# A mixture-of-experts layer on one NeuronCore: the width of an expert chosen in five places of TensorE's program instead of one

## The chip, the cores and the metric

One Trainium2 chip (trn2), one NeuronCore. The metric is the device time of one execution in microseconds. Three runs of the kernel before gave 617.49, 617.75 and 617.79 us, median 617.75.

## What is computed

x is 16 sequences of 128 tokens with 256 features in float32. Four blocks follow each other, each added to x through a tanh gate: a decaying retention over the context, a first mixture-of-experts layer, attention over the context, and a second mixture of experts. The change touches the first mixture of experts:

```python
def _moe_forward(x, Wg, W_in, W_out):            # E = 8 experts, K = 2 of them for a token, F = 512
    C = int(math.ceil(K * S / E * CAP_FACTOR))   # S = 2048 tokens: 640 places in each expert
    ...
    loc = jnp.take_along_axis(cum, flat_idx[:, None], axis=1)[:, 0]
    keep = loc < C
    buf = jnp.zeros((E, C + 1, h), x.dtype).at[e_flat, l_flat].set(xk)
    inp = buf[:, :C]
    hid = jnp.einsum('ech,ehf->ecf', inp, W_in)
    a, g = jnp.split(hid, 2, axis=-1)
    hid = jax.nn.gelu(a, approximate=False) * g
    out_e = jnp.einsum('ecf,efh->ech', hid, W_out)
```

## The kernel before, in words

Each engine has its own program, and they meet through semaphores. Layer 0 (the first mixture of experts) gathers the rows of each expert from DRAM into five tiles of 128 rows (POOL, `gather0`), turns them on TensorE (`xt0`), multiplies them with W_in (`hid0`) and the result with W_out (`out0`), and scatters the rows back (`scatter0`). Every product is made of three float32r matmuls over a high and a low part of both operands (`exact`, line 1542); ScalarE makes the high parts and VectorE the low ones.

On TensorE the eight experts are a loop of four passes with two experts in each (`Fori`, line 1616): par 0 has the even experts, par 1 the odd ones. `expert0` is one expert. An expert may have up to 640 rows, but if no more than 512 came to it, the last tile is empty and less work will do. So VectorE writes a flag for each expert into `full`; TensorE's queue loads the flag into a register (`value_load`, line 1607) and chooses between two copies of the expert's program:

- the wide copy: 8 hidden steps over 320 columns (12 matmuls each), and five output tiles of 12 matmuls;
- the narrow copy: 8 hidden steps over 256 columns, four output tiles of 12 matmuls, and one matmul for the fifth (line 1593), which only keeps the count of tiles.

In both copies the rows of the next expert are turned between the output tiles: tile 0, then the turned rows of pairs 0 and 1 (8 transposes), then tiles 1 and 2, then pair 2 (2 transposes, line 1554, which wait for VectorE to have read pair 0 of the same bank), then tiles 3 and 4. In memory the wide copy stands first and the narrow one behind it, and so for par 0, then for par 1. A wide expert runs its copy and jumps over the narrow one; a narrow expert jumps over the wide copy and goes on behind its own. Lines 1565, 1566, 1571, 1580, 1583 and 1584 are the waits in front of a step or a tile; where their count depends on the expert, they are register instructions in TensorE's queue.

```python
with pe.If(pe.value_load(full[0:1, bass.ds(e, 1)], min_val=0, max_val=1) > 0):
    run(HALF)
with pe.Else():
    run((CAP - P) // 2)
```

In this input experts 0, 3 and 7 are wide and 1, 2, 4, 5 and 6 narrow. Behind the loop TensorE goes on with the context of the attention, then the attention, then layer 1.

Of the kernel before, what the change touches and what calls it, by code (L numbers as in the profile page):

```python
# [30 lines left out]
P = 128  # L31
# [10 lines left out]
CAP = math.ceil(K * T / E * 1.25)  # L42
CT = CAP // P
# [5 lines left out]
HALF = CAP // 2  # L49
FB0 = F0 // P  # L50
FB1 = F1 // P
PIECES = 4
STEPS0 = 2 * FB0
# [47 lines left out]
def build(nc, x, ctxt, mask, g_xattn, g_ffn, wg0, w_in, w_out, wq, bq, wk, bk, wvT, wv, bvc, bv, wg1T, w1, w2, cf_d, out):  # L101
    with ExitStack() as ctx:
        def sb(name, shape, dt=F32):
            return ctx.enter_context(nc.sbuf_tensor(name, shape, dt))
# [80 lines left out]
        full = sb("full", [P, E], I32)  # L185
# [32 lines left out]
        def tiles_of(pair):  # L218
            return range(2 * pair, min(2 * pair + 2, CT))

        def bank0(pair):

            return PB[:, pair % 2, 0:len(tiles_of(pair)) * D].rearrange("p (t c n) -> p t c n", c=DC, n=P)
# [1164 lines left out]
        def _(pe):  # L1388
# [148 lines left out]
            def exact(dst, lhs_hi, lhs_lo, rhs_hi, rhs_lo, first=True, last=True):  # L1537

                n = len(lhs_hi)
                for k in range(n):  # L1540
                    for a, b in ((lhs_hi, rhs_hi), (lhs_hi, rhs_lo), (lhs_lo, rhs_hi)):
                        mm = pe.matmul(dst, a[k], b[k], start=(first and k == 0 and a is lhs_hi and b is rhs_hi),  # L1542
                                       stop=(last and k == n - 1 and a is lhs_lo))
                return mm


            def xt0(i, par, e, pair, between=None):
                if pair == 2:
                    pe.wait_ge(xt0_lo, e * PAIRS + 1)
                for t in tiles_of(pair):  # L1550
                    s = par * CT + t
                    pe.wait_ge(g0_in[s], i * 16 + 16)
                    for k in range(DC):
                        mm = pe.transpose(bank0(pair)[:, t % 2, k, :], xg[:, s, k * P:(k + 1) * P], ident)  # L1554
                    if t == tiles_of(pair)[-1]:
                        mm.then_inc(xt0_done, 1)
                    if between is not None:
                        between(t)

            def hid0(e, width):  # L1560

                for s in range(STEPS0):
                    half, fb = divmod(s, FB0)

                    pe.wait_ge(xt0_lo, e * PAIRS + PAIRS - 1 + half)
                    pe.wait_ge(hid0_used, e * STEPS0 + s + 1)
                    for n in range(2):
                        col = n * F0 + fb * P
                        for k in range(DC):
                            if s == 0 and n == 0:  # L1570
                                pe.wait_ge(win_lo[0], e * DC + k + 1)
                            mm = exact((PA, PC)[s % 2][:, n, 0:width],
                                       *([w[:, col + k * 2 * F0:col + k * 2 * F0 + P]] for w in (whi, wlo)),
                                       *([v[:, k, half * width:(half + 1) * width]] for v in (xhi, xlo)),
                                       first=k == 0, last=k == DC - 1)
                    mm.then_inc(hid0_done, 1)

            def out0(par, e, width, tiles_now):
                for t in tiles_now:
                    pe.wait_ge(wout_lo[0], e * 2 + 2)  # L1580

                    steps = FB0 if (t + 1) * P <= width else STEPS0
                    pe.wait_ge(h0_lo, e * STEPS0 + steps + 4)
                    pe.wait_ge(y0_evac, e * CT + t + 1)
                    bank = PD[:, (par * CT + t) % 2, 0:D]
                    if t * P < 2 * width:
                        at = t * P + (HALF - width) * (t * P // width)
                        exact(bank, *([h[:, f * CAP + at:f * CAP + at + P] for f in range(FB0)] for h in (hhi, hlo)),
                              *([w[:, WIN + f * D:WIN + (f + 1) * D] for f in range(FB0)] for w in (whi, wlo)))\
                            .then_inc(y0_done, 1)  # L1590
                    else:

                        pe.matmul(bank, hhi[:, 0:P], whi[:, WIN:WIN + D], start=True, stop=True).then_inc(y0_done, 1)

            def expert0(i, par, e):


                def run(width):
                    hid0(e, width)
                    out0(par, e, width, [0])  # L1600
                    xt0(i + par, 1 - par, e + 1, 0)
                    xt0(i + par, 1 - par, e + 1, 1)
                    out0(par, e, width, [1, 2])
                    xt0(i + par, 1 - par, e + 1, 2)
                    out0(par, e, width, range(3, CT))

                with pe.If(pe.value_load(full[0:1, bass.ds(e, 1)], min_val=0, max_val=1) > 0):
                    run(HALF)
                with pe.Else():
                    run((CAP - P) // 2)  # L1610

            for pair in range(PAIRS):
                xt0(0, 0, 0, pair, between=lambda t: values(1, [t]) if t < QB else None)
# [2 lines left out]
            with pe.Fori(0, E // 2) as i:  # L1616
                for par in range(2):
                    expert0(i, par, i * 2 + par)
# [190 lines left out]
```

## Time and profile before

| | |
|---|---|
| runs, median (lowest to highest) | 617.75 us (617.49 to 617.79) |
| profiled execution, its own time | 616.72 us |
| its span, first to last instruction | 614.7 us |
| mean granted TensorE clock | 0.921 of full speed |
| TensorE matmuls busy | 532.2 us, 87% |
| VectorE, ScalarE, POOL busy | 331.5, 304.0, 226.7 us |
| layer 0's experts on TensorE | from 81.70 to 251.9 us |

The span is what the profile shows; the execution's own time has 2.0 us around it. Times in the rows are microseconds from the span's start. PE is TensorE's matmuls, PEld its weight loads, and PEldq the queue that issues for both: register, wait and branch instructions stand there and are not counted as busy. The queue works ahead of the matmuls. "issue" is idle time for which the profile shows nobody to be waited for.

### The profile page before, as it was taken

What the parts mean: (1) busy time and instruction counts of PE and PEld (TensorE: products, weight loads), DVE (VectorE), ACT (ScalarE), POOL (GpSimd) and SP (SyncE); (2) the same over time, 40 slices, a digit from 0 to 9 for tenths busy, and PEclk for the clock granted to TensorE, in tenths of its full rate; (3) what the DMA queues carried; (4) which work ended last, traced back from release to release, by engine and by line L of the source; (5) the groups of instructions that cost most, each with busy time, mean ns of one, the idle gap of its engine ahead of it and who ended that gap; (6) DMA issues with size and microseconds to landing.
All of it is one profiled execution on the core that took longest, in us unless ns stands there. A gap on an engine that the chain in (4) does not pass through costs nothing.

```text
span 614.7 us, 12118 instructions
## 1 busy us (share of the span) xinstructions
PE 532.2 (87%) x3567; PEld 481.3 (78%) x3572; DVE 331.5 (54%) x817; ACT 304.0 (49%) x645; POOL 226.7 (37%) x256
## 2 busy tenths in 40 slices
PE   2796987899999999799891289999999999999991
PEld 1475877899999999777771178889898989898981
DVE  1878734356666675374858834544454445444520
ACT  3655335366656675426463435554555455545530
POOL 2300564345365450431000123535454435353531
PEclk9776599799999999979997579999999999999997
DMA  8943253144344434341122343645343544452231
GB/s 263 368 153 138 57 158 116 50 163 133 131 153 155 165 99 161 115 150 55 36 68 95 87 134 69 167 104 118 103 104 103 118 103 103 102 119 36 34 45 18
DMA packets 51726, 71.43 MB, mean 116 GB/s; under 512 B 7056, under 2 KB 43408, under 8 KB 51696
## 3 DMA queue, kind: packets, MB, share of 16 engines
q1 hardware_dynamic: 40752, 50.31, 24.8%
q0 software_dynamic: 10944, 20.76, 15.6%
q8 instruction: 14, 0.23, 0.2%
q14 instruction: 16, 0.13, 0.1%
HBM read 50.72 MB, written 20.33 MB: 116 GB/s over the span
## 4 chain that ended last, share of the span: by engine, by line
PE 70%; DVE 14%; issue 5%; ACT 3%; DMA 2%; SPq 1%; DVEq 1%; POOL 0%; ACTq 0%; POOLq 0%
PE PA L1542 25%; PE PD L1542 21%; PE PC L1542 8%; PE PC L1734 4%; PE PB L1399 3%; DVE stats L886 2%; PE PD L1399 2%; PE PB L1554 2%; DVE ys L1038 1%; DVE wlo L1159 1%; DMA xs<-x 1%; PE PA L1399 1%; ACT whi L746 1%; PE PB L1716 1%; PE PC L1399 1%
## 5 line engine op out<-in xcount | busy, mean ns | idle before, releaser
L1542 PE MATMUL PD<-whi,hhi 128*128 128x256 f32 x420 | 122.7, 292 | 0.0
L1542 PE MATMUL PD<-wlo,hhi 128*128 128x256 f32 x420 | 118.6, 282 | 0.0
L1542 PE MATMUL PD<-whi,hlo 128*128 128x256 f32 x420 | 118.5, 282 | 0.0
L554 POOL DMA_INDIRECT out<-ys,row_o x35 | 55.9, 1596 | 106.6 <-DVE ys L1350 106.3
L1542 PEld LDWEIGHTS PD<-wlo,hhi 128*128 128x128 f32 x420 | 80.1, 191 | 0.0
L1542 PEld LDWEIGHTS PD<-whi,hlo 128*128 128x128 f32 x420 | 80.1, 191 | 0.0
L1542 PEld LDWEIGHTS PD<-whi,hhi 128*128 128x128 f32 x420 | 79.9, 190 | 0.1
L481 POOL DMA_INDIRECT xg<-xn_rows,row_x x45 | 45.0, 1001 | 76.9 <-DVEq L1024 41.4
L844 ACT ACTIVATE hhi<-PC 128x512 fp32r<-128x512 f32 x70 | 38.1, 595 | 67.4 <-PE PC L1734 67.4
L534 POOL DMA_INDIRECT xg<-xn_rows,row_x x38 | 39.2, 1032 | 84.8 <-DMA xn_rows<-gate_rows 68.1
L839 ACT ACTIVATE xT<-PA 128x512 f32<-128x512 f32 x72 | 42.3, 599 | 49.8 <-PE PA L1542 49.5
L488 POOL DMA_INDIRECT y_rows<-ys,row_y x40 | 44.0, 1099 | 58.8 <-ACT ys L699 56.0
L1542 PE MATMUL PA<-whi,xhi 128*128 128x512 f32 x144 | 61.0, 423 | 2.9 <-DVE xlo L1159 2.9
L1542 PE MATMUL PA<-whi,xlo 128*128 128x512 f32 x144 | 57.4, 399 | 0.0
L1542 PE MATMUL PA<-wlo,xhi 128*128 128x512 f32 x144 | 56.8, 395 | 0.0
L1159 DVE TENSOR_TENSOR hlo<-PC,hhi 128x512 fp32r<-128x512 f32 x70 | 45.0, 685 | 14.5 <-ACT hhi L844 14.5
L1159 DVE TENSOR_TENSOR wlo<-raw,whi 128x512 fp32r<-128x512 f32 x64 | 40.0, 686 | 23.5 <-ACT whi L746 23.4
L1542 PE MATMUL PA<-xhi,whi 128*128 128x256 f32 (+1 forms) x128 | 38.7, 303 | 9.9 <-issue 7.3
L1350 DVE TENSOR_SCALAR ys<-PD,slot_gate 128x256 f32<-128x256 f32 x35 | 16.9, 484 | 52.7 <-PE PD L1542 45.4
L1159 DVE TENSOR_TENSOR xlo<-PB,xhi 128x256 fp32r<-128x256 f32 x37 | 15.7, 423 | 50.2 <-ACT xhi L834 48.2
L1122 DVE TENSOR_TENSOR ring<-ring,PA 128x320 f32<-128x320 f32 x32 | 15.6, 488 | 48.0 <-ACT ring L687 48.0
L1542 PE MATMUL PA<-xhi,wlo 128*128 128x256 f32 (+1 forms) x128 | 38.0, 297 | 0.0
(250 smaller groups left out, 1249.6 us busy)
## 6 DMA issues: line engine op xcount, KB each, us to landing
raw<-w SPq DMA_DIRECT2D x16, 1024.0 KB, 5.5
raw<-L_ffn_W_in SPq DMA_DIRECT2D x8, 1024.0 KB, 5.3
raw<-L_ffn_W_out SPq DMA_DIRECT2D x8, 512.0 KB, 3.6
y_rows<-ys SPq DMA_DIRECT2D x8, 512.0 KB, 7.1
xn_rows<-xn SPq DMA_DIRECT2D x8, 512.0 KB, 3.3
xs<-x SPq DMA_DIRECT2D x4, 512.0 KB, 7.8
cx<-ctx SPq DMA_DIRECT2D x4, 512.0 KB, 8.5
ys<-y_rows SPq DMA_DIRECT2D x4, 512.0 KB, 4.4
```

Source lines behind the costliest of these rows:

```text
L481: pool.indirect_dma_start(xg[:, s, :], None, xn_rows[0].ap(), bass.IndirectOffsetOnAxis(ap=row_x[:, e % E * CT + t:e % E * CT + t + 1], ax ...
L488: pool.indirect_dma_start(y_rows.ap(), bass.IndirectOffsetOnAxis(ap=row_y[:, e * CT + t:e * CT + t + 1], axis=0), ys[:, s, :], None).then_ ...
L534: pool.indirect_dma_start(xg1[j % 2], None, xn_rows[1].ap(), bass.IndirectOffsetOnAxis(ap=row_x[:, j:j + 1], axis=0)).then_inc(g1_in[j % 2 ...
L554: pool.indirect_dma_start(out, bass.IndirectOffsetOnAxis(ap=row_o[:, j:j + 1], axis=0), ys[:, j % 2, :], None, compute_op=ALU.add).then_in ...
L839: act.activation(h1[:, f * 512:(f + 1) * 512], PA[:, f, :], ACT.Silu).then_inc(silu_done, 1)
L844: act.activation(hhi[:, n * 512:(n + 1) * 512], PC[:, n, :], ACT.Copy).then_inc(ht1_hi, 1)
L1122: dve.tensor_tensor(ga[:, s % 4, :], ga[:, s % 4, :], (PA, PC)[s % 2][:, 1, 0:HALF], ALU.mult).then_inc(hid0_used, 1)
L1159: return dve.tensor_tensor(dst, src, hi.bitcast(F32), ALU.subtract)
L1350: dve.tensor_scalar(ys[:, par, :], PD[:, par, 0:D], slot_gate[:, bass.ds(j, 1)], None, ALU.mult)\
L1399: mm = pe.matmul(dst, a, b, start=(k == 0), stop=(k == len(lhs) - 1))
L1542: mm = pe.matmul(dst, a[k], b[k], start=(first and k == 0 and a is lhs_hi and b is rhs_hi), stop=(last and k == n - 1 and a is lhs_lo))
L1734: mm = pe.transpose(PC[:, n, b * P:(b + 1) * P], h1[:, f * P:(f + 1) * P], ident)
```

## The change

`hid0` gets the steps that it has to do as an argument. `expert0` loads the flag once and chooses by it in five places: hidden steps 0 to 3, hidden steps 4 to 7, output tile 0, output tiles 1 and 2, output tiles 3 and 4. The turned rows stand between them, once for both widths. The order of the matmuls of an expert stays as it was. The lines of the choice and the load are now 1598 (load), 1601 and 1607 (choices), and the loop is line 1625.

```diff
-            def hid0(e, width):
-
-                for s in range(STEPS0):
+            def hid0(e, width, steps_now):
+
+                for s in steps_now:
                     half, fb = divmod(s, FB0)
...
             def expert0(i, par, e):
 
 
-                def run(width):
-                    hid0(e, width)
-                    out0(par, e, width, [0])
-                    xt0(i + par, 1 - par, e + 1, 0)
-                    xt0(i + par, 1 - par, e + 1, 1)
-                    out0(par, e, width, [1, 2])
-                    xt0(i + par, 1 - par, e + 1, 2)
-                    out0(par, e, width, range(3, CT))
-
-                with pe.If(pe.value_load(full[0:1, bass.ds(e, 1)], min_val=0, max_val=1) > 0):
-                    run(HALF)
-                with pe.Else():
-                    run((CAP - P) // 2)
+                wide = pe.value_load(full[0:1, bass.ds(e, 1)], min_val=0, max_val=1)
+
+                def hidden(steps_now):
+                    with pe.If(wide > 0):
+                        hid0(e, HALF, steps_now)
+                    with pe.Else():
+                        hid0(e, (CAP - P) // 2, steps_now)
+
+                def output(tiles_now):
+                    with pe.If(wide > 0):
+                        out0(par, e, HALF, tiles_now)
+                    with pe.Else():
+                        out0(par, e, (CAP - P) // 2, tiles_now)
+
+                hidden(range(FB0))
+                hidden(range(FB0, STEPS0))
+                output([0])
+                xt0(i + par, 1 - par, e + 1, 0)
+                xt0(i + par, 1 - par, e + 1, 1)
+                output([1, 2])
+                xt0(i + par, 1 - par, e + 1, 2)
+                output(range(3, CT))
```

TensorE's program, before, at the end of the narrow copy of par 0, where par 1 begins: the last output tiles, the load of the flag, and the one choice, behind which the wide copy starts (PD holds the output tile, PA and PC the hidden products).

```order
L1593 MATMUL PD<-whi,hhi 128x256
L1609 UNCONDITIONAL_BRANCH
L1607 ISA
L1607 TENSOR_LOAD full
L1607 ISA x2
L1607 COMPARE_AND_BRANCH
L1565 ISA
L1566 ISA
L1571 ISA
```

With the change the same boundary has the same instructions (lines 1598 and 1601 for 1607), but the choice now jumps over four hidden steps, 48 matmuls of 320 columns, where it jumped over the whole wide copy of 166.

TensorE's program, before, narrow copy, from the end of output tile 2 over pair 2 of the turned rows to tile 3:

```order
L1542 MATMUL PD<-wlo,hhi 128x256
L1542 MATMUL PD<-whi,hlo 128x256
L1549 ISA
L1554 MATMUL PB<-cf,xg 128x128 x2
L1584 REGISTER_ALU
L1542 MATMUL PD<-whi,hhi 128x256
```

The same place with the change (the narrow piece; the wide piece of tile 3 and 4 stands in the same way behind the choice):

```order
L1542 MATMUL PD<-wlo,hhi 128x256
L1542 MATMUL PD<-whi,hlo 128x256
L1609 UNCONDITIONAL_BRANCH
L1549 ISA
L1554 MATMUL PB<-cf,xg 128x128 x2
L1607 COMPARE_AND_BRANCH
L1580 ISA
L1583 ISA
L1584 ISA
```

A branch has come in between the turned rows and the tile, and three register instructions (ISA) stand where a wait and one register instruction (REGISTER_ALU) stood.

## Rows read from the trace of the kernel before

**Rows 1.** The page, parts 1 and 3: busy time by engine, and the instruction queue.
```profile
PE 532.2 (87%) x3567; PEld 481.3 (78%) x3572; DVE 331.5 (54%) x817; ACT 304.0 (49%) x645; POOL 226.7 (37%) x256
...
q8 instruction: 14, 0.23, 0.2%
```

**Rows 2.** Stretches of layer 0, PE alone: stretch, length, busy (count), clock, DMA share, GB/s.
```profile
104.31:110.56 6.25, 0.00 (x0) 0.80 0.57 218
110.56:115.59 5.03, 5.03 (x26) 0.57 0.01 3
131.67:134.81 3.14, 3.14 (x26) 1.00 0.89 273
150.38:172.71 22.33, 22.33 (x167) 1.00 0.41 131
...
191.62:210.77 19.15, 18.72 (x155) 1.00 0.47 151
...
110.56:131.67 21.11, 20.61 (x155) 0.90 0.23 70
```

**Rows 3.** The chain of waits around the start of expert 1: start, length, what.
```profile
104.31 6.25 issue
...
115.59 1.44 PE PA L1542 x12
```

**Rows 4.** Timeline of VectorE, 101 to 103: expert 1's last operand.
```profile
102.36 0.42 DVE L1115 TENSOR_TENSOR xlo<-PB,xhi 128x256 fp32r<-128x256 f32 x1
```

**Rows 5.** Line 1607 in five short stretches: ns min/median/max, first and last start.
```profile
L1607 PEldq COMPARE_BRANCH  x1: 3306/3306/3306, 102.0 to 102.0; - x1
...
L1607 PEldq COMPARE_BRANCH  x1: 4047/4047/4047, 106.2 to 106.2; - x1
...
L1607 PEldq COMPARE_BRANCH  x1: 169/169/169, 170.7 to 170.7; - x1
...
L1607 PEldq COMPARE_BRANCH  x1: 208/208/208, 191.0 to 191.0; - x1
...
L1607 PEldq COMPARE_BRANCH  x1: 77/77/77, 229.0 to 229.0; - x1
```

**Rows 6.** DMA queues in 87.8:88.8, 102.9:103.9, 107.8:108.8 and 110.9:112: packets, MB.
```profile
q8 instruction: 1, 0.02, 5.7%
...
q8 instruction: 1, 0.02, 6.0%
...
q8 instruction: 1, 0.02, 6.1%
...
q8 instruction: 1, 0.02, 5.4%
```

**Rows 7.** All instruction queues in 116.8:253.8 (q14 is not TensorE's).
```profile
q14 instruction: 3, 0.02, 0.1%
```

**Rows 8.** The stretch between two code packets: PE and PEld busy (instructions), the other engines.
```profile
87.90:103.00 15.10, 15.10 (x117) 15.10 (x116) 9.57 (x18) 8.99 (x21) 6.46 (x7) 1.00 0.22 62
```

**Rows 9.** Timeline of the weight loads: the first of expert 4, behind expert 3.
```profile
172.71 0.19 PEld L1542 LDWEIGHTS PA<-xhi,whi 128*128 128x128 f32 x1
```

**Rows 10.** Lines 1565 and 1571 in 191:191.6, behind a taken choice.
```profile
L1565 PEldq FUSED_REGOPS  x1: 42/42/42, 191.3 to 191.3; - x1
L1571 PEldq FUSED_REGOPS  x1: 37/37/37, 191.5 to 191.5; - x1
```

**Rows 11.** How far the queue is ahead in expert 4: register and wait instructions, then matmuls.
```profile
L1583 PEldq EVENT_SEMAPHORE  x1: 51/51/51, 182.8 to 182.8; - x1
184.35 0.28 PE L1542 MATMUL PD<-whi,hhi 128*128 128x256 f32 x1
...
L1583 PEldq EVENT_SEMAPHORE  x2: 51/51/51, 189.2 to 189.5; - x2
189.68 0.36 PE L1542 MATMUL PD<-whi,hhi 128*128 128x256 f32 x1
```

**Rows 12.** Waits of the weight loads in 111:252: total us, times, longest.
```profile
PEld PA L1542 <- issue: 2.0, 5, 0.7
```

## The prediction, made before the changed kernel ran

> **What bounds the kernel now.** I first read the page: TensorE (PE) is busy 87% of the span, VectorE 54%, ScalarE 49% [rows 1]. That is an average, so the table of stretches comes next, cut at the eight experts of layer 0 [rows 2]. In each of the experts 1 to 7 the matmul time fills the stretch to within 0.5 us; three of the rows stand for them: wide expert 3 is 22.33 us of matmuls back to back, narrow expert 5 takes 19.15 us with 18.72 busy, expert 1 21.11 with 20.61. Nothing that VectorE, ScalarE or a transfer does shows in this stage; whatever delays TensorE there delays the end.
>
> Between expert 0 and expert 1 it stands still. The chain of waits has one piece named "issue" of 6.25 us at 104.31, the longest of the stage [rows 3], and the granted clock tells what follows: expert 1 begins at 0.57 mean, so at the 1.2 GHz level for most of its first 26 matmuls, which take 5.03 us, where the same 26 matmuls of expert 2 take 3.14 us at 1.00 [rows 2, 3]. No data is missing: the last operand of expert 1, xlo, was written from 102.36 on, for 0.42 us [rows 4].
>
> The rows of line 1607 say what "issue" is. Two branches are long: the jump from the end of the wide copy over the narrow one, 3306 ns from 102.0, and the choice that sends expert 1 to its narrow copy, 4047 ns from 106.2. The same jump after expert 3 takes 169 ns, and the same choice 208 ns for a narrow and 77 ns for a wide expert [rows 5]. In the middle of both long branches the instruction queue q8 moves one packet, 0.02 MB, at 102.9 to 103.9 and at 107.8 to 108.8 [rows 6]. So both branches waited for code. From 116.8 to 253.8 q8 moves nothing, though the loop runs three more times [rows 7]: the loop's code, once there, stays. The loss belongs to the first pass alone.
>
> How far apart is the code? Between the packets of 87.8 to 88.8 and of 102.9 to 103.9, TensorE ran 117 matmuls and 116 weight loads [rows 6, 8], with some 14 register and wait instructions by the program, so a packet carries about 250 instructions (estimate). Counting two instructions for a matmul, the jump of expert 0 passes over the narrow copy, 155 matmuls or 336 instructions, and the choice for expert 1 over the wide copy, 358 instructions. Both distances are more than one packet.
>
> **Removed.** The five choices cut the same program into pieces of at most 104 instructions; the longest jump is now one of these. A piece ahead is therefore in the packet that runs or in the next one. That the next is fetched ahead also after a jump shows behind the second long branch: q8 moves a packet at 110.9 to 112 [rows 6], while expert 1 still has some 80 instructions to go to the end of the packet it jumped into. From entering a packet to needing the next, the first pass has at least 5 us, and the longest wait for code is 4.05 us. So I take both long branches at their later values, 169 and 208 ns. Behind expert 3, also wide and followed by a narrow one, the first weight load of expert 4 has no idle time in front of it [rows 9]. The 6.25 us go down to 0.1 us: **-6.15 us**. Without standstill the clock has no reason to fall, as at none of the later boundaries [rows 2]: 5.03 becomes 3.14, **-1.89 us**. Together -8.04.
>
> **Added: four more choices for each expert.** A choice costs the queue that issues for TensorE about 0.3 us when taken (208 ns, and the next register instruction stands 0.3 us behind, 191.0 to 191.3), and each piece sets three registers for its waits, 0.1 us each (the first at 191.3, the third at 191.5) [rows 5, 10]; before, one or two such instructions stood there, 0.2 us. So 0.4 us in a narrow expert and, with 77 ns not taken, about 0.2 in a wide one. Whether TensorE feels it depends on how far its queue is ahead:
> - Behind the hidden products the wait of output tile 0 stands in the queue at 182.8, its first matmul runs at 184.35 [rows 11]. The lead is 1.6 us, a little more than one hidden step (12 matmuls in 1.44 us [rows 3]). The choices in front of tile 0 and of the second half of the hidden steps, 0.4 us each, are hidden.
> - Between the turned rows and output tiles 1 and 2 the queue has the 1.44 us of tile 0 and 0.87 us of turns to run ahead. Hidden.
> - In front of tile 3 it is not. The queue waits there for the last turned rows' bank, and is back at 189.2, 0.4 us ahead of the matmul at 189.68 [rows 11]. From there to the next expert it is the queue that sets the pace, since tile 4 of a narrow expert has one matmul: even now the five boundaries behind a narrow expert leave up to 0.7 us open, 2.0 us in all [rows 12]. So 0.4 us for each narrow expert: five times, **+2.0 us**. A wide expert has 24 matmuls there, 2.9 us to catch up: about 0.1 us each, three times, **+0.3 us**.
>
> The bounds of that term: nothing, if the lead covers all; and 1.0 us for a narrow and 0.3 for a wide expert, if the choice in front of tiles 1 and 2 shows too with its registers: 5.9 us. I take 2.3, by the rows at 189. The shared turned rows cost nothing and save nothing in time: each expert ran one copy of them anyway. The loop's code shrinks by 20 matmuls of 1400 instructions; nothing follows from that. The other engines' programs are the same, and they are ready: POOL, VectorE and ScalarE wait for TensorE in this stage. What comes behind the loop starts when TensorE gets there, so the gain stays.
>
> **Sum.** -8.04 + 2.3 = -5.7 us. The profiled execution took 616.72 us (span 614.7 and 2.0 around it), 1.0 us under the median of the three runs, 617.75. So 611.0 for a profiled execution, and **612.0** for the median.
>
> The Trainium skill bears on this in "Runtime: NRT & Kernel Launch", section "Instruction fetch mechanics". It says that code comes in blocks of 16 KiB, 256 instructions, and that TensorE's memory holds 2048; the trace agrees with the first (q8: 14 packets, 0.23 MB, on the page [rows 1]), and with the second as far as a loop of 1400 instructions stays. "Advanced Engine Details and Errata", section "ISA Cache", says "Only 2 cache lines!"; by that every pass of the loop would fetch again, the even flow of experts 2 to 7 would be impossible, and the loss to win would be far more than 8 us. The trace decides against it for TensorE [rows 7].
>
> **Rivals.**
> *The choices show (slower).* If no choice is hidden, 4 more of them in 8 experts are 32, and at 0.4 us more for 20 and 0.3 us for 12 they cost 11.6 us; with the branch at the end of each wide piece (169 ns, 12 times, 2.0) 13.6. Net +5.6: **623.3**. For it: the last boundary shows that the lead can be as small as 0.4 us. Against: the lead of 1.6 us inside the hidden products [rows 11]. The point where it decides is 8.04 / 32 = 0.25 us for each added choice.
> *Jumps stop the fetching ahead (slower).* Then each new packet of the first pass is waited for: five of them within the two experts, each up to 4.05 us less a lead of 1.6, about 2.5 us, so 12.3 us in place of 6.15, the clock still falls, and the choices cost their 2.3: +8.5, **626.2**. For it: the long jump ended at 105.3, and no packet followed before the choice of 106.2 asked for one. Against: the packet of 110.9, and that choice came within 0.8 us.
> The same page of the Trainium skill states it as a rule: prefetch is purely sequential, and "branching breaks sequential prefetch", which is why it would have straight code. By that rule five choices are worse than one, and this rival would be the likely one; a run of before shows only one packet that speaks against it.
> *Half of it.* One of the two waits for code stays somewhere in the first pass, behind a boundary of packets that I place only within 30 instructions. It leaves 2.5 us open, as above, and may keep the clock down: -8.04 + 2.5 + 1.89 + 2.3 = -1.35, **616.4**; with the clock kept up, -3.2, 614.5.
> *No gain.* The 6 us come back as a wait behind the loop. Nothing in the rows speaks for it, since each later stage starts from TensorE's end.
>
> **Chances.** The forecast 0.68, half of it 0.12, the choices show 0.10, no fetching ahead 0.06, no gain 0.04. A measurement of this kernel tells 0.2%, 1.2 us, from no change. Faster by more: forecast and half, 0.80; within: 0.05; slower: 0.15. The range starts at 609.4, where the choices cost nothing (617.75 - 8.04 = 609.7, and 0.3 for the runs' spread), takes in the forecast with the highest price of the choices (617.75 - 8.04 + 5.9 = 615.6) and the half case, to 616.5. What lies outside, the slower rivals and no gain, is 0.20.
>
> **What the profile would show.** Right: no branch over 0.3 us in the expert stage, eight choices and four times as many more at 208 or 77 ns; between expert 0 and 1 under 0.5 us; clock 1.00 from expert 0 to the end of the stage; the same number of q8 packets, 14, none of them within a long branch; narrow experts about 0.4 us longer, from the first to the last 5.7 us shorter. Wrong: a branch of 3 or 4 us left in the first two experts (half, or no fetching ahead), or gaps of 0.2 to 0.6 us in front of the second half of the hidden products and of output tiles 0 and 1 (the choices show).

## The result, and the profile after

The changed kernel takes **612.21 us** (median of 6 runs, 609.38 to 614.46), the kernel before it, run beside it, 617.33 us (6 runs). The ratio is 0.9927, 95% interval 0.9898 to 0.9956. In two more comparisons, each on a chip of its own and with 5 to 19 runs a side, the same pair gave 0.9887 [0.9855, 0.9919] and 0.9916 [0.9885, 0.9947]. In microseconds the three differences are 5.1, 8.1 and 4.1, mean 5.8, where 5.7 was forecast. Each has an interval of about 2 us to both sides, so the closeness of the mean is in part luck. The sum behind the forecast did not come out: one term of it turned out to be nothing, and in each of the three pairs of profiles 1.9 to 2.9 us are given back behind the stage, in a place that the prediction didn't name.

The profiled execution took 609.38 us. Its page, parts 1 and 3, against [rows 1]:
```profile
PE 536.6 (88%) x3567; PEld 484.5 (80%) x3572; DVE 332.7 (55%) x817; ACT 303.5 (50%) x645; POOL 227.1 (37%) x256
...
q8 instruction: 14, 0.23, 0.2%
```
TensorE has the same 3567 matmuls, and the instruction queue moves the same 14 packets.

The two groups of choices in the first expert layer: line 1601 chooses for the hidden steps, line 1607 for the output tiles (ns min/median/max):
```profile
L1601 PEldq COMPARE_BRANCH  x21: 73/208/313, 82.4 to 232.1; - x21
L1607 PEldq COMPARE_BRANCH  x33: 65/183/337, 89.8 to 240.5; - x33
```
54 branches, none over 0.337 us (a 55th, the first of all, ends before the stage starts and is short too). The 3306 and 4047 ns of [rows 5] are gone.

The chain of waits around the start of expert 1 (start, length, what), against [rows 3]:
```profile
97.04 0.22 PE PB L1554 x2
97.26 2.88 PE PD L1542 x24
100.13 1.44 PE PA L1542 x12
```
The piece of 6.25 us named "issue" is gone too, and expert 1's first hidden step takes 1.44 us at once, as that of expert 2 did before.

The experts, one stretch each (length, PE busy, count, clock, DMA share, GB/s), against [rows 2]:
```profile
99.97:119.77 19.80, 19.02 (x158) 1.00 0.42 145
119.77:139.12 19.35, 18.95 (x155) 1.00 0.48 150
139.12:161.57 22.45, 22.45 (x168) 1.00 0.44 131
```
In these three the clock stays at 1.00. In expert 0 it does not (23.99 us at a mean of 0.93, where 1.00 was forecast): it is at half its level from 77.1 to 80.5, which before didn't have and which costs about 1.5 us, as shown below. The whole stage, 75.98 to 242.76, takes 166.8 us against 170.4 before (81.70 to 252.06 there): 3.6 us gained in this pair of profiles, not 5.7. Three things were therefore open: whether distance is what made the two branches long, whether the choices cost something (narrow expert 2 takes 19.35 us here and 18.71 in the trace of before), and where the rest is.

### The profile page after: what moved, and what is told of

Its sections match the earlier page's. It is cut to its first block, busy times and chain, and to the rows that moved or that the text cites. A ratio compares the mean times of both kernels' runs of the same rounds, so it can differ in the third digit from the quotient of the medians.

```text
span 607.4 us, 12186 instructions
## 1 busy us (share of the span) xinstructions
PE 536.6 (88%) x3567; PEld 484.5 (80%) x3572; DVE 332.7 (55%) x817; ACT 303.5 (50%) x645; POOL 227.1 (37%) x256
## 4 chain that ended last, share of the span: by engine, by line
PE 67%; DVE 17%; issue 6%; ACT 4%; DMA 2%; SPq 1%; DVEq 1%; POOL 0%; POOLq 0%; ACTq 0%
PE PA L1542 24%; PE PD L1542 21%; PE PC L1542 8%; PE PC L1743 3%; DVE stats L886 3%; PE PB L1399 2%; PE PD L1399 2%; PE PB L1554 2%; DVE ys L1038 2%; DVE xs L1173 1%; DVE wlo L1159 1%; PE PB L1725 1%; PE PA L1399 1%; DMA xs<-x 1%; DVE xs L1209 1%
## 5 line engine op out<-in xcount | busy, mean ns | idle before, releaser
L1542 PE MATMUL PC<-xhi,whi 128*128 128x256 f32 (+1 forms) x128 | 38.1, 297 | 0.4 <-DVE ring L1122 0.4
```

## The experiments

Theory: a branch is long when it goes to code further off than the packet fetched ahead, and only in the first pass. Rival for the branches: any rearrangement of the code would do. Rival for the choices, which is the prediction's term: each narrow expert pays 0.4 us for them.

### One choice, but the narrow copy first

```diff
-                with pe.If(pe.value_load(full[0:1, bass.ds(e, 1)], min_val=0, max_val=1) > 0):
+                with pe.If(pe.value_load(full[0:1, bass.ds(e, 1)], min_val=0, max_val=1) < 1):
+                    run((CAP - P) // 2)
+                with pe.Else():
                     run(HALF)
-                with pe.Else():
-                    run((CAP - P) // 2)
```

> One choice per expert as before, but the narrow copy stands first in the program and the wide one behind it. Theory (code): the long branches of the first pass come from jumping over more than the next packet of code. Expert 0 is wide and now runs the second copy, so its end falls straight into the load for expert 1, and expert 1 is narrow and goes straight on. No branch over 0.3 us, no standstill at expert 1, clock 1.00 there: the stage of the eight experts takes 170.4 - 8.0 = 162.3 us, each narrow expert 18.7 to 19.2 us as before, and the time is about 609.5 us. Rival (first use): code that runs for the first time costs its wait wherever it stands, or the standstill has another cause at that moment (the weights' transfers). Then a standstill of 4 to 6 us stays between expert 0 and 1 and the time stays within 2 us of 617.3.

Measured: 616.45 us, ratio 0.9976 [0.995, 1.0002], so nothing that can be told from no change, where about 609.5 had been expected. The long branches between experts 0 and 1 are gone as expected (the longest is 368 ns), but the chain of waits has a new piece inside expert 0:
```profile
81.33 0.53 PE PC L1542 x2
81.86 2.54 issue
84.40 2.83 PE PC L1542 x10
87.23 2.81 PE PA L1542 x12
```
TensorE stands still in the second hidden step, and the next 22 matmuls run at the half level of the clock, where it had been since 79.2. The jump into the wide copy is at 77.7. TensorE can run 14 matmuls of it and then lacks code, so the jump landed close to the end of a packet, and the next packet begins only at 81.9. The table of stretches says what the DMA engines did meanwhile (PE, PEld, DVE, ACT, POOL busy; clock, DMA share, GB/s):
```profile
78.00:79.00 1.00, 0.59 (x4) 0.59 (x5) 0.00 (x0) 0.00 (x0) 1.00 (x1) 1.00 0.98 397
79.00:80.00 1.00, 1.00 (x6) 1.00 (x5) 0.00 (x0) 0.00 (x0) 1.00 (x2) 0.60 1.05 430
...
81.00:82.00 1.00, 0.86 (x4) 0.73 (x3) 0.17 (x1) 0.44 (x1) 1.00 (x1) 0.50 1.11 373
82.00:83.00 1.00, 0.00 (x0) 0.00 (x0) 0.32 (x1) 0.00 (x0) 0.25 (x1) 0.50 0.11 28
```
They are full with the weights of the next expert until 82, and the packet moves when they are through. My expectation had looked at distance alone. This gave a second cause to test: the packet waits behind the weights.

### More and fewer choices

Three kernels on the same chip divide the work otherwise. Hidden steps whole, so four choices for an expert:
```diff
-                hidden(range(FB0))
-                hidden(range(FB0, STEPS0))
+                hidden(range(STEPS0))
```

> The change with one choice for all eight hidden steps, so four choices per expert. In the changed kernel each narrow expert stands still 0.57 us in the second half of its hidden steps, where the signal of one step (hid0_done) comes 1.1 us behind its last matmul instead of 0.3. Theory: that delay comes with the choice in the middle of the hidden steps. It goes: narrow experts 18.7 to 18.9 us where the changed kernel has 19.4 to 19.8, the stage 2.9 us shorter, about 609.3 us. Rival: every choice costs its share in the queue, 0.65 us over four added ones: narrow experts 0.16 us shorter only, 0.8 us in all. The pieces of 206 instructions are still shorter than a packet, so no long branch.

Two choices, one around the hidden steps and one around all outputs, which have the turned rows in each copy again:
```diff
+                def outputs(width):
+                    out0(par, e, width, [0])
+                    xt0(i + par, 1 - par, e + 1, 0)
+                    xt0(i + par, 1 - par, e + 1, 1)
+                    out0(par, e, width, [1, 2])
+                    xt0(i + par, 1 - par, e + 1, 2)
+                    out0(par, e, width, range(3, CT))
...
+                for part in (lambda w: hid0(e, w), outputs):
```

> Two choices per expert: hidden steps, and all output tiles with the turned rows inside both copies. Longest jump 206 instructions. Theory (code): no branch over 0.4 us in the first pass, no standstill at expert 1, and nothing late in the hidden steps: narrow experts as before (18.7 to 19.2 us), about 609.3 us. Rival: pieces of this length reach the end of the packet sooner than the next one is there, so that one branch of 1 us or more stays in experts 0 or 1, about 611.

The hidden steps in four, so seven choices:
```diff
-                hidden(range(FB0))
-                hidden(range(FB0, STEPS0))
+                for s in range(0, STEPS0, 2):
+                    hidden(range(s, s + 2))
```

> The change with the hidden steps in four pieces of two, so three choices inside them instead of one. Theory (a choice inside the hidden steps delays a signal): each of the three costs a narrow expert up to 0.57 us: narrow experts 20.0 to 21.1 us, wide ones as before since their steps leave 0.3 us more; the stage 3 to 6 us longer than the changed kernel's, 615 to 618 us. Rival (the delay belongs to one step of the expert, whatever the choices): narrow experts stay at 19.4 to 19.8 us and the time at 612.

Measured, beside 617.22 us for before:

| choices | time | ratio | experts' stage | longest branch |
|---|---|---|---|---|
| 2 | 610.59 | 0.9888 [0.9842, 0.9934] | 167.6 us | 2624 ns |
| 4 | 608.21 | 0.9862 [0.9817, 0.9906] | 168.4 us | 2167 ns |
| 7 | 609.91 | 0.9889 [0.9845, 0.9933] | 166.8 us | 337 ns |

The intervals overlap, and the three can't be ranked. Two readings follow. Two and four choices still leave one long branch, so not every rearrangement does it, and the rival written down for the kernel with two choices is what came. The branch is the choice of expert 1's hidden steps, behind the load of its flag; line 1609 in the kernel with two choices, and the instruction queue in 99.8:100.71, just before it starts:
```profile
L1609 PEldq COMPARE_BRANCH  x2: 286/1455/2624, 99.5 to 100.7; - x2
```
```profile
q8 instruction: 1, 0.02, 9.8%
```
In 100.71:103.4, while it waits, the queue moves nothing. So the packet that it waits for was on its way before the branch began, and the branch jumps over 206 instructions only, less than a packet. Distance is not the cause of this one. It is time: the jump of 286 ns before it had just entered a packet, at 99.8, the next packet starts 0.8 us later, at 100.6, and is of use only at 103.3. In the kernel with four the packet starts at 99.6 and the branch of 2167 ns at 100.15. TensorE stands still for 1.9 and 1.2 us there, where it was 6.25 in before.

And seven choices are not slower than four, where 615 to 618 us had been expected. The branches of the kernel with seven (44 at the hidden steps, where the change has 21):
```profile
L1601 PEldq COMPARE_BRANCH  x44: 67/188/312, 78.9 to 235.4; - x44
L1607 PEldq COMPARE_BRANCH  x33: 65/179/337, 93.2 to 243.8; - x33
```
The narrow experts 2, 4 and 6 take 19.4 to 19.5 us in the three kernels, and 19.6 to 19.8 in the one with a single choice on the same chip. That is 0.7 over the 18.7 of expert 2 in the trace of before, but it does not grow with the number of choices. My expectation for the kernel with four, that the delay would go, failed too. Their waits name the place, in the kernel with seven:
```profile
PE PA L1542 <- DVE ring L1122: 1.7, 4, 0.5
PE PA L1542 <- issue: 0.6, 2, 0.3
PE PC L1542 <- DVE ring L1122: 0.4, 1, 0.4
```
Once in each narrow expert, inside the hidden steps, the hidden products wait for VectorE (the two rows with it, five times in all). In the trace the semaphore of the fifth hidden step arrives there 1.0 to 1.15 us behind the start of the step's last matmul, and that of every other step 0.3 us. Whether the change has any part in that needed before and after side by side.

### Before and after, twice more

The two kernels unchanged, on a second and on a third chip.

> The kernel before, unchanged, profiled together with the runs below. In the first profile of it no hidden step stood still, while the changed kernel and four variants of it, also the one with a single choice (e1), stand still 0.5 to 0.6 us once in each narrow expert. Theory (the choices cost it): here too no standstill inside the hidden steps, narrow experts 18.7 to 19.2 us. Rival (it belongs to the execution, not to the change): 0.5 to 0.6 us in the hidden steps of the narrow experts here as well, 19.3 to 19.9 us each, and then the added choices cost next to nothing. In both: two long branches of 3 to 4 us between expert 0 and 1.

> The changed kernel, unchanged, beside it: no branch over 0.4 us in the expert stage, expert 0 to 1 without standstill, clock 1.00 from expert 1 on, eight experts in 165 to 167 us; 6 to 9 us less than the stage of the kernel before in the same call. The time 0.987 to 0.993 of before.

> The kernel before, unchanged, as the partner of the two kernels beside it on the same chip. Ratio 1.000, 614 to 617.5 us; between expert 0 and expert 1 two long branches of 3.3 to 4.1 us, the first expert layer 169.5 to 171 us. It also tells apart two readings of the 0.5 to 0.6 us standstill inside the hidden steps of each narrow expert: if it belongs to the chip or the execution, it shows here whenever it shows in the changed kernel beside it; if the small choices made it, it never shows here (narrow experts of 18.7 us).

> The changed kernel, unchanged. My theory by now: no long branch in the first expert layer, the added choices cost nothing that can be measured, so about 8 us less than before: ratio 0.986 to 0.991, the layer 162 to 164 us. The rival, the reckoning of the prediction with 0.4 us for each narrow expert: 5.7 us less, ratio 0.991, the layer 164 to 165.5 us with narrow experts of 19.1 to 19.4 us while the kernel before beside it has 18.7.

The first of these two is called the second chip below (the four kernels above ran on one chip of their own, and which chip the first pair ran on isn't on record). There: before 613.73, after 606.65, ratio to the 19 runs of before (614.72) 0.9887 [0.9855, 0.9919]. Narrow expert 2, before and then after:
```profile
128.57:147.28 18.71, 18.71 (x155) 1.00 0.49 155
```
```profile
122.47:141.16 18.69, 18.69 (x155) 1.00 0.49 155
```
Third chip: before 616.32, after 612.28, ratio to the 19 runs of before (616.39) 0.9916 [0.9885, 0.9947]. The same expert, before and then after:
```profile
128.90:148.24 19.34, 18.97 (x155) 1.00 0.46 150
```
```profile
122.88:142.23 19.35, 18.99 (x156) 1.00 0.47 150
```
This settles the choices. On the second chip neither kernel has the wait inside the hidden steps, on the third **both** have it, also the kernel without the added choices. It belongs to the chip or the execution. And within one chip the lengths of the narrow experts 2, 4, 5 and 6 are the same in both kernels to 0.06 us. Over experts 2 to 7 on the third chip, where 24 choices were added, before takes 122.73 us (the lengths 19.34, 22.44, 19.30, 19.75, 19.29 and 22.61) and after 122.70; on the second 120.38 and 120.23. The added choices cost 0.0 us, to about 0.1. The stage's length missed the ranges written down for it: 163.35 us in after on the second chip (165 to 167 expected), and 172.97 and 164.88 on the third (169.5 to 171, and 162 to 164). So did the ratio on the third chip, 0.9916 where 0.986 to 0.991 had been written down for a cost of nothing.

The stage on the third chip takes 172.97 us before and 164.88 after: **8.1 us** less, of which 6.35 in expert 0 with the standstill behind it and 1.71 in expert 1. On the second it is 6.6 us. There the first stretch of after's expert 0 shows why it isn't 8.1; the second row is the third chip's:
```profile
79.35:103.33 23.98, 23.98 (x166) 0.93 0.37 116
```
```profile
80.70:103.15 22.45, 22.45 (x167) 1.00 0.42 111
```
On the second chip the clock was at half its level from 80.6 to 84.0, just behind the start of the stage, which costs 1.5 us. Of the twelve profiles told of here without the block of the next section, six have such a stretch: the first of after, this one, the kernels with four and with seven choices, the one with the narrow copy first, and the kernel before with a late transfer, below. That is four of six with added choices and two of six with a single one, too few to say whether the choices have a part in it.

### A distance of more than a packet, put in on purpose

238 matmuls that never run are set between the hidden steps and output tile 0 of even experts, so that a choice must jump over 477 instructions in each pass. The bound of the flag's load is raised to 2, so that the new condition isn't decided beforehand:
```diff
-                wide = pe.value_load(full[0:1, bass.ds(e, 1)], min_val=0, max_val=1)
+                wide = pe.value_load(full[0:1, bass.ds(e, 1)], min_val=0, max_val=2)
...
+                if par == 0:
+                    with pe.If(wide > 1):
+                        for n in range(238):
+                            pe.matmul(PD[:, 0, 0:D], hhi[:, 0:P], whi[:, WIN:WIN + D], start=True, stop=True)
```
The flag is 0 or 1, so nothing that is computed changes.

> The changed kernel with a piece of 238 matmuls (477 instructions) that never runs, between hidden products and output tile 0 of the even experts. Theory (code packets of 256 instructions, the next one fetched when one is entered): the jump over it goes from instruction 1006 to 1484, two packets on, right after the packet of 1006 was entered, so in expert 0 it waits about 3 us: one branch of 2.5 to 4 us at 90 us, of which 1 to 2.5 us show on TensorE. The loop is then eight packets long: if eight stay, experts 2, 4 and 6 show nothing; if not, the same branch is long again in each of them. Rival (the long branches of before had to do with the load of the flag or with the change of expert, not with distance): no branch over 0.4 us anywhere.

Measured in a single execution: 643.43 us against 614.72. The jump over the block (line 1615), the loop's jump back (line 1629) and the instruction queue:
```profile
L1615 PEldq COMPARE_BRANCH  x4: 208/5048/6240, 90.1 to 244.1; - x4
```
```profile
L1629 PEldq COMPARE_BRANCH  x3: 3437/3457/3637, 124.6 to 223.7; - x3
```
```profile
q8 instruction: 36, 0.59, 0.4%
```
The first of the four, in expert 0, took 6240 ns, where after has no branch over 0.337 us: in the first pass a distance of more than a packet is enough to make a long branch, since nothing but never-run code was added. It is more than the 2.5 to 4 us expected; two packets move meanwhile, the first only 2.2 us into it, and why so late is open. Those in experts 2 and 6 took 5163 and 4933 ns, but the one in expert 4 took 208 ns over the same distance, and no packet moves from 182 to 219: a far jump costs nothing when the code is there. The block did more than I wanted, since the loop, now some 1850 instructions long, no longer stays as a whole: 36 packets instead of 14, and a wait of 3.4 to 3.6 us at each turn of the loop. The 29 us are therefore not the price of four jumps, and the run says nothing on that price.

### Does the packet wait behind the weights?

First in the kernel before: the transfer of expert 2's W_in, which fills the DMA engines during the second long branch, is held until expert 1 has done its second hidden step.
```diff
+                    if e == 2 and first:
+                        sp.wait_ge(hid0_done, STEPS0 + 2)
```

> The kernel before, with the transfer of expert 2's W_in (1 MB, issued at 102.5, in the middle of the standstill) held back until expert 1's second hidden step is done. Theory (the code packet queues behind the weights on the DMA engines: in before it starts at 107.9, when they fall idle, 1.7 us after it was wanted): both branches stay long, but the second takes 2.5 to 3.1 us instead of 4.05 and the standstill is 1 to 1.5 us shorter; stage and time 1 to 2 us shorter. Rival (fetching code takes 3 to 4 us by itself): both branches as before, the time the same.

Measured: 612.38 us, ratio 0.9976 [0.9941, 1.001], not to be told from none. The branches show what the time doesn't (line 1609 here is line 1607 of before):
```profile
L1609 PEldq COMPARE_BRANCH  x2: 2107/2904/3701, 101.1 to 105.8; - x2
```
The second branch falls to 2107 ns, from 4047 [rows 5], and from 3407 on the same chip. The standstill falls from 6.1 to 4.8 us; waits of TensorE in 98:112, the kernel before and then this one:
```profile
PE PA L1542 <- issue: 6.1, 1, 6.1
```
```profile
PE PA L1544 <- issue: 4.8, 1, 4.8
```
So some 1.3 us of the second long branch was the packet's turn in the DMA engines.

This trace also shows what the second branch waits for. It starts at 105.8. The instruction queue in 104.8:105.77, before it:
```profile
q8 instruction: 1, 0.02, 6.3%
```
In 105.77:107.9, while it waits, the queue moves nothing. So here too the target lay in a packet already on its way, which starts 0.75 us behind the end of the first long branch, and not in one further off. In before the same packet starts 2.6 us behind the end of the first long branch, in its two repeats 2.1 and 2.2, with the DMA engines at a share of 1.0. In all four the branch ends 1.3 to 1.4 us after the packet has moved. The first long branch is another case: its packet starts about 1.0 us after the branch does. So of the two, the first is the one that distance made long. The second is long because it comes about 1 us after a packet was entered, while the next is of use only 3.0 us after that, or 4.4 to 4.9 us with the weights in the way.

Then the sharper test: the kernel with one choice and the narrow copy first, with the weights out of the way of the packet that came late there. SyncE issues in order, so W_out's transfer, behind W_in's, is held too; both are issued after 82 there.
```diff
+                    if e == 1 and first:
+                        sp.wait_ge(hid0_done, 3)
```

> The kernel with one choice around all products and the narrow copy first, which stood still for 2.5 us in expert 0's second hidden step, with one thing more: the transfer of expert 1's W_in is not started until expert 0's third hidden signal. Theory (the packet of code waited in the DMA engines behind the transfers of the weights): with the weights out of the way the packet arrives at 79 to 80 us instead of 82, the standstill shrinks to under 0.5 us, TensorE's clock doesn't fall to half again after it, and the time is 607 to 610 us, ratio 0.986 to 0.991, with a single choice. Rival 1 (the packet is late by the instructions' own fetching, whatever the DMA engines carry): the standstill stays at 2 us or more and the time at ratio 0.996 to 1.000, as without the wait. Rival 2: the other transfer (W_out, issued 0.5 us later on the same engines) holds the packet as long; then too the standstill stays, and the DMA engines' share stays near 1 to 82 us.

Measured on the third chip: **609.25 us, ratio 0.9899 [0.9864, 0.9935]**, with a single choice, where it had 0.9976 without the wait (on another chip). The stretches and the chain around the old standstill:
```profile
78.00:79.00 1.00, 1.00 (x9) 1.00 (x8) 0.00 (x0) 0.00 (x0) 0.98 (x2) 1.00 0.22 57
79.00:80.00 1.00, 0.96 (x7) 0.84 (x6) 0.00 (x0) 0.29 (x1) 1.00 (x1) 1.00 0.47 86
80.00:81.00 1.00, 0.45 (x4) 0.45 (x4) 0.49 (x1) 0.14 (x1) 1.00 (x2) 1.00 0.04 12
```
```profile
79.67 0.29 PE PC L1544 x2
79.96 0.59 issue
80.55 1.62 PE PC L1544 x10
```
The packet moves at 78.1, 1.2 us behind the jump and at a DMA share of 0.2, instead of 4.2 us behind it at a share of 1.0; the standstill falls from 2.54 to 0.59 us (under 0.5 had been expected), and the clock stays at 1.00 (part of the gain may be that the stage here began without the half-clock stretch of 79.2, which the transfer can't be shown to have caused). The theory holds for the packet and the standstill. Rival 1 is out. Rival 2, W_out by itself, was not told apart, since both transfers moved.

One small thing remains for the single choice. With the narrow copy first, a narrow expert ends on a jump over the wide copy, just in front of the load of the next expert's flag. Its narrow experts 2, 4 and 6 take 19.72, 19.54 and 19.70 us, those of before and after on that chip 19.29 to 19.35.

## Why the prediction was right, and where it was not

**What bounds.** Right. TensorE's queue waited for code in two branches. The instruction queue, the distance put in, and the late transfer all say so. What it missed is that it put both branches down to a distance of more than one packet. That holds for the first. The second jumped into the packet that was already coming, and waited because it came too soon after the first, and 1.3 us longer because the weights were in the DMA engines. The change removes both cases, and so the price of the removal held.

**Removed: -6.15 and -1.89.** Right. On the third chip, where no half clock falls at the start of the stage, the stage loses 8.09 us: 6.35 in expert 0 with the standstill, 1.71 in expert 1, and 0.03 in all others. The forecast was 6.15 and 1.89, together 8.04. In the other two pairs the stage lost 3.6 and 6.6 us. 1.5 us of the difference is each time the half clock in expert 0, where 1.00 was forecast; about 3 us more in the first pair are the late semaphore in the narrow experts, which its profile of after has and its profile of before has not.

**Added: +2.3.** This is the step that failed. The prediction put the choice in front of tile 3 behind the wait at 189.2, with the queue 0.4 us ahead, and took 0.4 us for each narrow expert. It measured 0.0. The wait at line 1583 that I read there as that for the turned rows' bank is that of the output tiles, which stands *behind* the choice in the program. In after the choice (line 1607) is taken at 181.7 and a wait of line 1583 comes at 182.3, while the last matmul of tile 2 starts at 181.84; the third chip's rows:
```profile
L1607 PEldq COMPARE_BRANCH  x1: 208/208/208, 181.7 to 181.7; - x1
```
```profile
L1583 PEldq EVENT_SEMAPHORE  x1: 51/51/51, 182.3 to 182.3; - x1
```
From tile 1's first matmul to the next expert's first it is 4.97 us there (179.00 to 183.97) and 4.98 before (185.01 to 189.99). And the queue comes to the load of the next expert's flag at the same moment in both, 3.59 us behind tile 1's first matmul; before, then after:
```profile
L1607 PEldq FUSED_REGOPS  x2: 51/101/151, 188.6 to 189.1; - x2
```
```profile
L1598 PEldq FUSED_REGOPS  x2: 37/94/151, 182.6 to 183.1; - x2
```
Between its last wait and that load the queue has nothing of its own to do for 0.53 us in before and for 0.13 us in after: the choice costs the queue the 0.4 us that I had reckoned, but it had them to spare, although it was only 0.4 us ahead of tile 3. So the wrong step is the sentence that from there on the queue sets the pace. From the load of the flag to the next first matmul it is 1.27 us before and 1.28 after, which the change didn't touch. What holds the queue in that gap no row tells. The lower bound that the prediction gave for this term, "nothing, if the lead covers all", is the value.

**"The gain stays."** Only in part, in the three pairs of profiles. Something is given back behind the stage each time. From the end of the stage to the first scores' products of the following attention (line 1666 of before, 1675 of after) the two kernels take:

| profiles | before | after |
|---|---|---|
| first pair | 28.4 us | 32.1 us |
| second chip | 28.8 us | 30.3 us |
| third chip | 27.9 us | 32.2 us |

The work is the same. The chain of waits on the third chip, before:
```profile
256.53 5.52 PE PD L1399 x32
...
262.42 1.68 DVE xs L1173 x4
...
264.12 2.09 DVE xs L1173 x4
...
274.03 3.70 PE PB L1399 x8
```
And after:
```profile
250.46 7.01 PE PD L1399 x32
...
257.84 2.39 DVE xs L1173 x4
...
260.26 2.50 DVE xs L1173 x4
...
270.57 5.40 PE PB L1399 x8
```
5.52 becomes 7.01 and 3.70 becomes 5.40: these are stretches in which the granted clock is at its half level, 250.4 to 260.6 and 270.9 to 274.3 in after, only 258.2 to 265.0 in before. VectorE's eight operations take 1.1 us more; why is open. Together 4.3 us. Before has a half-clock stretch at 306.0 to 309.4 that after lacks, so up to the second expert layer the loss is 2.6 us (103.4 against 106.1 us from stage to stage; 1.9 in the first pair and 2.9 on the second chip). The kernels with two, four and seven choices take 101.1 to 103.5 us there and so don't show it, though their stages end at about the same time. So it isn't a price of short choices as such. Nor is it a matter of when the stage ends: that is 245.6 in after on the third chip, which shows the loss, and in the kernel with four choices, which doesn't. Chance in three profiles is not ruled out.

**Sum.** Stage and what lies behind it, up to the second expert layer, come to -1.7 us in the first pair of profiles (-3.6 and +1.9), -3.7 on the second chip (-6.6 and +2.9) and -5.5 on the third (-8.1 and +2.6), where the medians of the runs differ by -5.1, -8.1 and -4.1. So a pair of profiles doesn't give the difference of the runs: one profile stands for one execution, and the one of after on the second chip, 609.22 us, is the slowest of its five. The prologue alone varies as much: the stage starts at 81.7, 79.0 and 78.7 in before and at 76.0, 79.4 and 80.7 in after. What can be said is that the forecast's -8.04 was right for an execution without the half clock in expert 0, that its +2.3 stood at the wrong place, and that the match of 5.7 and 5.8 is luck so far as it rests on what happens behind the stage, which nobody had reckoned.

**Rivals.** "The choices show": out, 8 x 7 choices are as fast as 8 x 4. "Jumps stop the fetching ahead": out. After has five packets within the first two experts, and no branch waits for any; behind the second long branch of before, which ends at 110.2, the next packet starts at 111.0. The Trainium skill, "Runtime: NRT & Kernel Launch", section "Instruction fetch mechanics", says that branching breaks sequential prefetch, and explains it by a taken branch whose target isn't in the current window of two pages: it has to wait until that page is there. The first long branch of before (3306 ns) and the jump over the block (6240 ns) agree with this. What the prediction read out of the rule, that five choices are worse than one, doesn't follow from it and isn't what the runs show. "Half of it", a wait for code left somewhere, didn't happen in the change, but did in the kernels with two and four choices and, by another way, in the one with the narrow copy first.

Of the signs named for the profile, the 14 packets outside any long branch, the standstill under 0.5 us and the clock from expert 1 on came true. The clock in expert 0 (0.93) and the narrow experts' 0.4 us did not, and the longest branch is 337 ns where 0.3 us was the bound.

## What to carry to other kernels

A branch that takes microseconds in the first pass of a loop and 0.2 us in later ones waits for code: look for the instruction queue's packets beside it, then cut the copies so that each jump lands within the packet ahead, leave time between entering a packet and needing the next (3.0 to 3.5 us here with the DMA engines free), and keep large transfers off them while the packet is due. 24 short choices more cost nothing here, because TensorE's queue had 0.5 us to spare in front of the boundary; so look for the queue's gaps there, and not only at how far it is ahead. Compare kernels stage by stage on one chip, and read the stage behind the change as well: in three profiles 1.9 to 2.9 us of the gain were lost there.

## What the runs showed that I had not expected

- Packets of code share the DMA engines with the weights. With the engines at a share of 1.0, a packet came 4.2 us behind the jump that needed it; at a share of 0.2 it came 1.2 us behind. Moving one transfer took the branch of 3407 ns to 2107.
- A jump over less than a packet can be long too: 2624 ns over 206 instructions, because the packet ahead had only just been asked for.
- There is a size of loop that stays: about 1400 instructions ran three more passes with no packet [rows 7], about 1850 fetched some again in each, 36 packets for 14.
- A semaphore of TensorE can come 1.0 us behind the start of its matmul instead of 0.3, once in each narrow expert: in the first profile of after, in the four kernels of the choices' chip and in all on the third, whatever their choices, but not in the first profile of before, and in none of the three on the second chip without the block. It costs 0.6 us an expert. Its cause is open; it isn't the number of choices.
- The clock can be at half its level just behind a stage's start, after the wait ahead of it: for 3.4 us, with 1.5 us lost, in five of twelve profiles, and for 10.2 us, around the standstill, in the one with the narrow copy first. What decides it is open.
